# Eight PSUM banks shared out anew: two instead of three for attention scores, five instead of four for everything else that is turned over in a ring

## The reference

```python
x = embeddings                                   # (8, 1024, 512) fp32
q, k, v = split(x @ w_qkv)                       # 16 heads of 32
probs = softmax(q @ k.T / sqrt(512))             # 1024 x 1024 per head
x = layernorm(x + heads(probs @ v))
g, u = fp4_linear(x, w_gate), fp4_linear(x, w_up)     # 512 -> 1408
x = layernorm(x + fp4_linear(silu(g) * u, w_down))    # 1408 -> 512
```

## Time and profile before

| | us |
|---|---|
| median of 3 runs | 3920.85 |
| lowest, highest | 3920.46, 3924.07 |
| the profiled execution, device time | 3922.93 |
| its span in the trace | 3921.3 |
| PE, DVE, POOL, ACT busy | 3744.5, 3024.0, 2232.0, 1709.7 |

### The profile page before, as it was taken

One profiled execution on the slowest core, in us unless ns is written; L12 is line 12 of the kernel. 1 busy time (PEld: TensorE's weight loads), 2 busy tenths in 40 slices (PEclk: granted clock), 3 DMA queues, 4 the chain that ended last, 5 costly groups with the idle time before them and its releaser, 6 DMA issues. The chain is left out here.

```text
span 3921.3 us, 61535 instructions
## 1 busy us (share of the span) xinstructions
PE 3744.5 (95%) x22853; PEld 1727.3 (44%) x22853; DVE 3024.0 (77%) x5075; ACT 1709.7 (44%) x3085; POOL 2232.0 (57%) x1427
## 2 busy tenths in 40 slices
PE   3599999999999999999999999999999999999999
PEld 2244454344544355443544445434454334544354
DVE  9876787678876688667877678767887668866787
ACT  2166423663246532555226542366424553255522
POOL 1298624984268832787229862398425883278722
PEclk9699999999999999999999999999999999999999
DMA  5211101011011110111101110101101111010110
GB/s 169 81 36 34 55 21 37 17 43 48 25 31 32 35 47 20 43 27 35 47 20 39 31 57 20 39 17 42 49 22 33 30 37 46 20 42 25 31 52 22
DMA packets 106565, 152.53 MB, mean 39 GB/s; under 512 B 28176, under 2 KB 55568, under 8 KB 106128
## 3 DMA queue, kind: packets, MB, share of 16 engines
q1 hardware_dynamic: 106256, 148.49, 12.2%
HBM read 76.28 MB, written 19.66 MB: 24 GB/s over the span
## 5 line engine op out<-in xcount | busy, mean ns | idle before, releaser
L604 DVE TENSOR_REDUCE mx<-R 128x1 f32<-128x512 f32 x2080 | 1316.9, 683 | 536.1 <-PE R L698 533.1
L1265 ACT ACTIVATE arena<-SC 128x512 f32<-128x512 f32 x1360 | 755.6, 603 | 407.9 <-PE SC L1531 279.2
L1606 PE MATMUL SC<-wgu,split 128*128 128x512 f16 (+1 forms) x3456 | 714.5, 361 | 0.0
L1176 POOL TENSOR_TENSOR arena<-arena,sc_h 128x704 f32<-128x704 bf16 (+1 forms) x144 | 178.0, 1250 | 606.1 <-DVE arena L528 606.1
L1150 POOL TENSOR_TENSOR wd<-wd,arena 128x1024 f32<-128x1024 f32 x212 | 494.2, 2358 | 44.5 <-ACT arena L1265 44.5
L1606 PEld LDWEIGHTS SC<-wgu,split 128*128 128x128 f16 x3456 | 338.3, 98 | 331.4
L1265 ACT ACTIVATE wd<-SC 128x512 f32<-128x512 f32 x688 | 389.8, 603 | 211.8 <-PE SC L1531 149.1
L1307 ACT ACTIVATE arena<-SC,gain 128x512 f32<-128x512 f32 (+1 forms) x192 | 125.1, 651 | 810.2 <-PE R L1606 411.9
L678 PE MATMUL R<-xT,wqkv 128*128 128x512 bf16 x1632 | 421.5, 380 | 19.5 <-DVE xT L591 13.1
L698 PE MATMUL R<-ks_even,qs_even 96*128 96x512 bf16 x1056 | 395.0, 389 | 27.6 <-DVE mx L604 7.8
L698 PE MATMUL R<-arena 96*128 96x512 bf16 x1024 | 374.0, 382 | 13.2 <-DVE xT L591 8.2
(11 more groups left out here) (138 smaller groups left out, 5496.6 us busy)
## 6 DMA issues: line engine op xcount, KB each, us to landing
x<-n_L_attn_embeddings_dram SPq DMA_DIRECT2D x136, 256.0 KB, 2.8
wd<-wd_kept SPq DMA_DIRECT2D x32, 512.0 KB, 5.4
out_dram<-x SPq DMA_DIRECT2D x64, 256.0 KB, 2.0
ks_even<-split SPq DMA_DIRECT2D x204, 64.0 KB, 2.0
qs_even<-split SPq DMA_DIRECT2D x408, 32.0 KB, 1.8
arena<-split SPq DMA_DIRECT2D x192, 64.0 KB, 2.0
arena<-split SPq DMA_DIRECT2D x384, 32.0 KB, 1.8
wd<-wd_kept SPq DMA_DIRECT2D x16, 384.0 KB, 7.2
```

Source lines behind the costliest of these rows:

```text
L604: nc.vector.reduce_max(mx[:, j:j + 1], ring_of(ring, job)[:, :], AX_X).then_inc(max_done, 1)
L1176: nc.gpsimd.tensor_tensor(blocks_of(q_h[:, cols]), blocks_of(r_h[:, cols]), spread(sc_h[:, c], c.stop - c.start), ALU.mult).then_inc(qh_do ...
L1265: nc.scalar.activation(probs_of(s)[:, hd, :], SC[e % SLOTS][:, :], ACT.Exp, scale=SCALE).then_inc(exp_done, 1)
L1606: last = nc.tensor.matmul(GU[kk % 2][which][:, 0:w], xhT[i % 2][:, part_x * KH + k, :], wgu[:, part_w * KH + k, which * I + first:which * ...
```

## The change

SLOTS goes from 3 to 2 and RING from 4 to 5. In the FFN phase the second pair of gate and up products now stands in the ring's last two banks instead of SC[2] and the ring's last one, and both are waited for. Between batches the planner hands the ring these two banks back ahead of the others. Nothing is computed otherwise, and no engine's order of instructions changes.

```diff
--- before.py
+++ after.py
@@ -46,8 +46,8 @@
 BATCHES = 4
 STEPS = UNITS * TILES
 BUFS = 3
-RING, RING_FFN = 4, 2
-SLOTS = 3
+RING, RING_FFN = 5, 2
+SLOTS = 2
 BANK = 512
 HALVES = S // BANK
 SCALE = 1.0 / float(H) ** 0.5
@@ -207,9 +207,10 @@
         turn, held, last_in, self.last_in = deque(range(slots)), None, {}, []
         for b, (jobs, ffn) in enumerate(batches):
             if b > 0:
-                turn.appendleft(slots - 1)
+                turn.extendleft(range(ffn_slots + 1, slots))
                 turn.append(ffn_slots)
-                last_in[slots - 1], last_in[ffn_slots] = ("gate", b - 1, 0), ("y", b - 1, 0)
+                last_in.update({slot: ("gate", b - 1, 0) for slot in range(ffn_slots + 1, slots)})
+                last_in[ffn_slots] = ("y", b - 1, 0)
             for n, (kind, a, j) in enumerate(jobs + ffn):
                 if n == len(jobs):
                     turn = deque(slot for slot in turn if slot < ffn_slots)
@@ -356,7 +357,7 @@
         SC = [pb(f"SC{n}", [P, BANK], F32) for n in range(SLOTS)]
         CT = pb("CT", [P, BANK], F32)
         R = [pb(f"R{i}", [P, BANK], F32) for i in range(RING)]
-        GU = [(SC[0][:, :], SC[1][:, :]), (SC[2][:, :], R[RING - 1][:, :])]
+        GU = [(SC[0][:, :], SC[1][:, :]), (R[RING - 2][:, :], R[RING - 1][:, :])]
         Y = [CT[:, :], R[RING_FFN][:, :]]
 
         def kept(t):
@@ -1597,8 +1598,8 @@
                         first, w = CHUNKS[c]
                         if c == 0 and which == 0:
                             pe.wait_ge(xhT_done, i + 1)
-                        if i % TILES == 0 and c == 1 and which == 1:
-                            released(*ring.last_in[i // TILES][RING - 1])
+                        if i % TILES == 0 and c == 1:
+                            released(*ring.last_in[i // TILES][RING - 2 + which])
                         if kk >= 2 and which == 0:
                             pe.wait_ge(h_done, kk - 1)
                         for k in range(KH):
```

## The result

The changed kernel takes 3998.5 us (median of four runs, 3998.1 to 4000.7) against 3922.5 us for the kernel before: a ratio of 1.0194, 95% interval 1.0179 to 1.0208. It is slower by 76 us. Forecast were 4014 us and a range of 3958 to 4072.

The account below looks back on a forecast made before the run. PE was taken to set the time in the eight batches. (19.0 - 8.3) x 8 = 85.6, plus 1.7 and 6, gave 93 us on 3920.85: 4014 us, 2.4% slower, range 3958 to 4072.

Parts of the forecast that it names:

- PE is the bound: In the eight batches, about 3,727 of 3,921 us, PE sets the time, so its waits are lost time.
- Score waits, 19.0 us a batch: Unit phases: each score now waits for the exponential two before; 19.0 us a batch lost, bounds 17.5 and 28.7.
- the second example: Unit phase, ACT copies a projection between exponentials: the third score would start 0.87 us late.
- Ring waits, 8.3 us won: Unit phases: a fifth bank removes PE's late starts of ring jobs; 8.3 us a batch won, bounds 5 and 8.9.
- FFN start, 1.7 us: FFN phase: chunk 1 products wait for DVE to read the context result, 0.85 us, twice, 1.7 us lost.
- The weight stage, put at 0: Weight stage: a bank more gains nothing, as DVE is full; taken as 0, bounds 0 and 3 us won.
- Clock, 6 us: More idle PE at unit ends makes clock dips likelier: three more at 2 us, 6 us lost; none at the least.
- The first two: Rivals: lateness once bought lasts, score cost 7.7 us a batch, 3913 us, chance 7%; or half that, 13 us, 3961, 9%.
- The third: Rival: the fifth ring bank brings nothing, its gain taken by the next score wait; 4081 us, chance 9%.
- The fourth: Rival: each score shortfall in the unit phases is paid, 28.7 us a batch; 4087 us, chance 6%.
- The fifth, the clock's swing: Rival: three more clock dips in each batch, 48 us in place of 6; 4056 us, chance 6%.
- the forecast case: Score cost 17.5 to 21 us, ring gain 7 to 8.9, dips none to eight: 3985 to 4040 us, chance 63%.

Follow-up runs that it names:

- e1: Kernel before with score tiles in two banks, the third left to the gate and up products alone, the ring kept at four: 4029.9 us.
- e5: Changed kernel with ACT's copies out of ring banks placed behind the exponential of their place, not ahead of it: 4009.1 us.
- e7: Changed kernel with one quarter of a projection moved from tile 1 to tile 7 in units 0 to 4: 3980.7 us.
- e9_after_refilled: Changed kernel with a step's first maximum ahead of its first score, and projection quarters dealt anew, more in tiles 6 and 7: 3959.5 us.

## Why the prediction was right, step by step

**PE is the bound.** Right. Every us of start excess came out as a us of the phase, in the changed kernel (10.7 against 10.5) and in e1 (13.7 against 13.9 us, 271.6 less 257.7).

**Score waits, 19.0 us a batch.** Right: 19.4 more than before (22.3 against 2.9). Taking the largest shortfall of each stretch of ACT, with the small addition for the two-bank cycle, gave the right sum; each shortfall for itself would have given 28.7. The waits are not the 41 that were counted but 72 late starts, as a shortfall can be paid in parts (0.12 and 0.76 us in the second example). That example named ACT's copy alone as the cause of 0.87 us. Its own rows say less: without the copy the exponential could have started 0.42 us after its score, at 2614.98 and not at 2615.32, so 0.34 us are the copy's; the other 0.53 are the cycle of 1.08 us less the 0.55 that PE needed to its second score after. e5 puts 0.27 of such a wait of 0.79 on the copy and leaves 0.52, which only PE's missing work between the scores of tile 7 explains; with more work there, and the copy later as well, the wait is gone (e7).

**Ring waits, 8.3 us won.** As a difference right: the other side fell by 8.7 us within the phase, and by 9.4 with the first row, which stands ahead of the phase's first score and which the prediction counted here. As a price of the fifth bank wrong: 4.5 us of it came with the score waits (e1), and only 3.4 us of phase length (271.6 to 268.2) are the bank's; of the 31 us of the whole that makes 27. The prediction did not see that its two terms act on each other. The sum was right all the same since it needed the difference of both edits and not the share of each.

**FFN start, 1.7 us.** Right: 0.84 us in two batches, forecast 0.85. Not forecast: the first maximum of a batch,'s first row, stands before the first score, so its 0.69 us is won in the stretch between the phases: four of these are 0.7 us shorter, and the two with the context wait only 0.1 us longer. In sum these stretches are 2.6 us shorter, where 1.7 us longer was forecast. The weight stage, put at 0, is 1.5 us shorter, which is no more than the spread of the kernels with four ring banks (193.1 to 196.4 us to the first score).

**Clock, 6 us.** Wrong: three more dips were forecast and none came. In its profiled execution the changed kernel has no dip inside a unit phase apart from the one at the turn between the rounds, which every kernel here has and which reaches 3.7 us into the fifth batch's; that of the kernel before had two more, and its two phases are some 2.4 us longer for it. Over all executions the mean clock is the same, 0.989 in 35 of the kernel before and in four of the changed one, so the two dips belong to this pair of traces and are no gain of the change. The clock is most of why the sum was too high, 93 us against 75.7 in the spans: 11 us of the difference are the clock's (6 forecast, some 5 the other way), 6 those of the FFN and weight stages, 1 the unit phases' waits. The unit phases together are 79.9 us longer, where 8 x 10.7 less the two dips gives 81. In the spans, 79.9 less 2.6 in the FFN phases and 1.5 in the weight stage are the 75.7 us between 3921.3 and 3997.0.

**Rivals.** The first two (a bought lateness lasts) fell: score waits rose by 19.4 us a batch, where they allowed 8.7 and 13, and the waits of a unit return in later tiles. The third fell in part: the fifth bank brings 3.4 us a phase, less than half of the 8.3 that were counted, but not nothing. The fourth fell by the measured 22.3 us. The fifth, the clock's swing, did not show: the Trainium skill's rule (TensorE: Matmul & The Clock Gate, "A second HAM failure mode: psum-queue depth-cycling") names small idle times from cycling banks; here 86 late starts in the phase shown left the mean clock at 1.00. The terms named for the forecast case add up to 3991 to 4050 us and not to 3985 to 4040; the measured time lies in both.

**A better version.** None of these beats the kernel before. The best with two and five, 3944 us, is 0.4 to 0.7% slower than it.

## What to carry to other kernels

Count for each PSUM ring the time from freed bank to freed bank (here 0.06 + 0.42 + 0.60 us for scores) and lay it beside the work that PE has between a product and the next user of its bank; waits appear where that work is short, not where the mean is. When two rings compete, change one at a time: waits at one let the other recover, so the gain of a bank is less than the waits that it could remove. An order written by hand is tuned to its number of banks: the same move of one job was worth -38 us with one split and +15 us with the other.

## What the hardware did that was not expected

The clock did not follow the sum of PE's idle time. The changed kernel waits 25 us in the unit phase shown, in pieces of at most 1.2 us, and keeps the higher level throughout; so it does in five others of its eight phases, and in the first and fifth, which follow the weight stage and the turn between the rounds, the mean is 0.99. e9_after_refilled is 21 us late in the phase shown, products slowed by the clock included, and its clock fell twice: behind a wait of 0.80 us at 2543.14 that follows one of 0.33 at 2541.95, and behind 0.59 and 1.36 us at 2774.37 and 2776.12. These are waits close together, as ahead of the dips of the kernel before (0.42 us at 1349.89 and 1.09 at 1351.87; 0.42 at 3217.15 and 1.22 at 3219.25). Two such waits 9 us apart in the changed kernel (0.74 at 2772.31, 1.04 at 2781.43) had no dip behind them. That closeness is what counts was only seen, not tried.
